# Causal linear attention: running sums over pairs of even and odd tokens, the even token's own term added from GpSimd

## The reference

```python
q, k = _rope(q, k); q = _phi(q); k = _phi(k)          # phi(x) = elu(x) + 1
def step(carry, qkv):
    K_sum, KV = carry
    q_t, k_t, v_t = qkv
    K_sum = K_sum + k_t
    KV = KV + k_t[..., :, None] * v_t[..., None, :]
    num = jnp.einsum('bhd,bhde->bhe', q_t, KV)
    den = jnp.maximum(jnp.einsum('bhd,bhd->bh', q_t, K_sum), EPS)
    return ((K_sum, KV), num / den[..., None])
```

## Time and profile before

| | us |
|---|---|
| median of 3 runs | 368.7 (367.78 to 368.82) |
| the profiled execution: its own time | 367.48 |
| its span | 365.7 |
| TensorE busy | 347.7 (95%) |
| VectorE busy | 317.6 (87%) |
| ScalarE busy | 276.1 (75%) |
| GpSimd busy | 204.3 (56%) |

### The profile page before, as it was taken

How to read it: one execution, slowest core, us unless ns; L and a number is a source line. 1 busy time by engine, 2 the same in 40 slices (tenths; PEclk the granted TensorE clock), 3 DMA queues, 4 the chain that set the end, 5 groups by cost and what they waited for, 6 DMA issues and landing times.

```text
span 365.7 us, 9318 instructions
## 1 busy us (share of the span) xinstructions
PE 347.7 (95%) x2534; PEld 299.9 (82%) x2534; DVE 317.6 (87%) x623; ACT 276.1 (75%) x774; POOL 204.3 (56%) x239
## 2 busy tenths in 40 slices
PE   7999988799899999999999899999999899999986
PEld 2788534499799999999999799989989688788875
DVE  3998799559989999999699979998996799998665
ACT  3887967777686877787878767787895987778752
POOL 3899118844234465756665648675857448883110
PEclk9999999999999999999999999999999999999999
DMA  6842848555355555655654554756642102221112
GB/s 182 217 124 74 325 192 234 173 149 134 108 133 137 139 143 146 170 139 150 175 143 135 152 161 129 186 150 152 148 115 70 31 2 57 57 61 29 30 29 59
DMA packets 45521, 47.00 MB, mean 129 GB/s; under 512 B 6928, under 2 KB 33712, under 8 KB 45216
## 3 DMA queue, kind: packets, MB, share of 16 engines
q1 hardware_dynamic: 40288, 36.88, 33.6%
q0 software_dynamic: 4320, 8.86, 11.5%
q10 hardware_dynamic: 864, 0.67, 0.7%
HBM read 32.88 MB, written 13.50 MB: 127 GB/s over the span
## 4 chain that ended last, share of the span: by engine, by line
PE 76%; DVE 14%; issue 3%; ACT 3%; DMA 2%; ACTq 1%; DVEq 0%
PE banks L546 16%; PE banks L534 14%; PE banks L674 6%; PE banks L675 6%; PE banks L330 3%; PE banks L983 3%; PE banks L1010 2%; PE banks L299 2%; PE banks L524 2%; PE banks L1039 2%; PE banks L321 2%; PE banks L1019 2%; PE banks L993 2%; PE banks L1057 2%; DVE cq L686 2%
## 5 line engine op out<-in xcount | busy, mean ns | idle before, releaser
L468 POOL DMA_INDIRECT xg<-xn_rows,slot_tok x71 | 74.8, 1053 | 74.2 <-PE banks L524 61.7
L563 ACT ACTIVATE xT<-banks,b1T 128x128 f32<-128x128 f32 x284 | 81.1, 371 | 15.4 <-PE banks L534 14.7
L546 PE MATMUL banks<-w_sb,xT 128*128 x568 | 79.6, 283 | 0.0
L485 POOL DMA_INDIRECT qk_exp<-expert_rows,ranki x64 | 63.7, 996 | 21.6 <-issue 17.9
L534 PE MATMUL banks<-xgT,w 128*128 128x128 f32 x568 | 75.3, 276 | 0.0
L546 PEld LDWEIGHTS banks<-w_sb,xT 128*128 128x128 f32 x568 | 69.3, 192 | 1.2
L534 PEld LDWEIGHTS banks<-xgT,w 128*128 128x128 f32 x568 | 69.0, 192 | 0.0
L686 DVE TENSOR_TENSOR cq<-banks,phi 128x360 f32<-128x360 f32 (+1 forms) x96 | 47.4, 548 | 19.1 <-PE banks L675 18.9
L652 ACT CAST high<-outer 128x1152 fp32r<-128x1152 f32 x32 | 37.1, 1158 | 21.6 <-DVE outer L641 21.2
L658 DVE TENSOR_TENSOR low<-outer,high 128x1152 fp32r<-128x1152 f32 x32 | 43.3, 1352 | 3.2 <-ACT high L652 3.2
L695 DVE TENSOR_REDUCE sums<-cq 128x144 f32<-128x1152 f32 x32 | 42.9, 1341 | 0.0
(11 more groups left out here) (205 smaller groups left out, 702.7 us busy)
## 6 DMA issues: line engine op xcount, KB each, us to landing
w<-in_L_ffn_W SPq DMA_DIRECT2D x71, 256.0 KB
expert_rows<-ye SPq DMA_DIRECT2D x71, 64.0 KB
expert_rows<-x_sb SPq DMA_DIRECT2D x2, 2048.0 KB, 10.6
x_sb<-in_L_attn_x SPq DMA_DIRECT2D x8, 256.0 KB, 4.3
xn_rows<-xn SPq DMA_DIRECT2D x8, 256.0 KB, 2.3
w_sb<-in_L_ffn_W SPq DMA_DIRECT2D x8, 256.0 KB, 4.5
out<-outer SPq DMA_DIRECT2D x7, 256.0 KB, 2.3
xg<-xn_rows,slot_tok POOLq DMA_INDIRECT x71
```

Source lines behind the costliest of these rows:

```text
L468: pool.indirect_dma_start(out=xg[n][:, :], out_offset=None, in_=xn_dram, in_offset=bass.IndirectOffsetOnAxis(ap=slot_tok[:, j:j + 1], axis ...
L485: pool.indirect_dma_start(out=y_moe[:, i, k, :], out_offset=None, in_=y_dram, in_offset=bass.IndirectOffsetOnAxis(ap=ranki[:, 0, k, i:i + ...
L546: last = nc.tensor.matmul(y, hidT[p][:, c, :], w2_sb[:, ds(e * NC + c, 1), :], start=False, stop=(c == NC - 1))
L563: last = nc.scalar.activation(hidT[p][:, c, :], ps[3 + p][:, c * P:(c + 1) * P], ACT.Gelu_apprx_tanh, bias=b1T[:, ds(e * NC + c, 1)])
```

## The change

Tokens are dealt out in pairs. Partition p of batch b now holds tokens 2p and 2p + 1: tile 2b has the even tokens, tile 2b + 1 the odd ones. The outer products of both are added (`attn_pair`), and there is one `high` and one `low` per batch, of that pair sum. An odd token needs all pairs up to its own: `tri_r`, 6 matmuls. An even token needs all pairs ahead of its own, `tri_x`, 6 matmuls, and its own product alone. That last part is (q . k) times (v, 1), which GpSimd computes in five small instructions (`attn_own`, into one of two buffers) and VectorE adds to the even tile's reduced sums (`attn_add_own`).

The feature map `phi` of the next batch moves from the end of the odd tile into the even tile's step, as do both outer products and the pair sum; `low` moves behind the sums of the odd tile. `high` is issued in the odd tile's step. x, its normalised copy and the output are moved by DMA with a pair of tokens in one line (1024 bytes where it was 512). In the second layer the blocks of a batch are swapped (`block_of`) and `mix` takes four instructions instead of two. GpSimd's and VectorE's moments share semaphores between the layers.

```diff
+    put("token_no", n // 2 * T + 2 * row + n % 2 - TOK // 2)
...
+    def by_tile(a, b, n):
+        return a.rearrange("(b p r) d -> p b (r d)", p=P, r=2)[:, b:b + n, :]
...
     def attn_outer(v, b, r, p):
...
-            v.wait_ge(high_ready, b * 2 - 1 + r)
-            v.wait_ge(low_ready, b * 2 - 1 + r)
+            v.wait_ge(high_ready, b)
+            v.wait_ge(low_ready, b)
+            v.wait_ge(pair_ready, b)
...
-    def attn_high(act, b, r, p):
-        i = b * 2 + r
-        act.wait_ge(outer_ready, i + 1)
-        act.wait_ge(den_ready, i + 1)
-        if from_(b, 2 - r):
-            act.wait_ge(cum_ps, b * 2 - (0 if r else 2))
-        nc.scalar.copy(high[kept(r, p)], outer[r]).then_inc(high_ready, 1)
-
-    def attn_low(v, b, r, p):
-        v.wait_ge(high_ready, b * 2 + r + 1)
-        n = kept(r, p)
-        nc.vector.tensor_tensor(low[n], outer[r], high[n].bitcast(f32), ALU.subtract).then_inc(low_ready, 1)
+    def attn_pair(v, b):
+        v.wait_ge(outer_ready, 2 * b + 2)
+        v.wait_ge(den_ready, 2 * b + 2)
+        nc.vector.tensor_tensor(outer[0], outer[0], outer[1], ALU.add).then_inc(pair_ready, 1)
+
+    def attn_high(act, b, p):
+        act.wait_ge(pair_ready, b + 1)
+        if b >= 2:
+            act.wait_ge(cum_ps, 2 * b - 2)
+        nc.scalar.copy(high[p], outer[0]).then_inc(high_ready, 1)
+
+    def attn_low(v, b, p):
+        v.wait_ge(high_ready, b + 1)
+        nc.vector.tensor_tensor(low[p], outer[0], high[p].bitcast(f32), ALU.subtract).then_inc(low_ready, 1)
+
+    def attn_own(pool, b, p):
+        pool.wait_ge(phi_ready, b + 1)
+        if b >= 2:
+            pool.wait_ge(own_used, b - 1)
+        nc.gpsimd.tensor_tensor(own_qk[:, :], phib[p][:, 0, 0:D], phib[p][:, 0, D:2 * D], ALU.mult).then_inc(own_part, 1)
+        q = own_qk[:, :].rearrange("p (h d) -> p h d", d=DH)
+        n = 4 * b + 1
+        for half in (DH // 2, DH // 4):
+            pool.wait_ge(own_part, n)
+            nc.gpsimd.tensor_tensor(q[:, :, 0:half], q[:, :, 0:half], q[:, :, half:2 * half], ALU.add).then_inc(own_part, 1)
+            n += 1
+        pool.wait_ge(own_part, n)
+        nc.gpsimd.tensor_tensor(own_dot[:, :], q[:, :, 0], q[:, :, 1], ALU.add).then_inc(own_part, 1)
+        pool.wait_ge(own_part, n + 1)
+        pool.wait_ge(ones_ready, 1)
+        nc.gpsimd.tensor_tensor(own[p][:, :, :], own_dot[:, :].unsqueeze(2).broadcast_to([P, H, E9]),
+                                qkv3[:, 2 * b, 2 * D:NW].rearrange("p (e h) -> p h e", h=H), ALU.mult).then_inc(own_ready, 1)
+
+    def attn_add_own(v, b, p):
+        v.wait_ge(own_ready, b + 1)
+        v.wait_ge(sums_ready, 2 * b + 1)
+        nc.vector.tensor_tensor(sums[:, 0, :, :], sums[:, 0, :, :], own[p][:, :, :], ALU.add).then_inc(own_used, 1)
...
     def attn_cumsum(pe, b, r, p):
-        pe.wait_ge(low_ready, i + 1)
-        parts = [(tri_r, kept(r, p))] + ([(ones_r, kept(0, p))] if r else [])
+        pe.wait_ge(low_ready, b + 1)
+        w = tri_r if r else tri_x
...
-            for m, (w, at) in enumerate(parts):
-                nc.tensor.matmul(o, w[:, :], high[at][:, cols], start=(m == 0), stop=False)
-                last = nc.tensor.matmul(o, w[:, :], low[at][:, cols], start=False, stop=(m == len(parts) - 1))
+            nc.tensor.matmul(o, w[:, :], high[p][:, cols], start=True, stop=False)
+            last = nc.tensor.matmul(o, w[:, :], low[p][:, cols], start=False, stop=True)
...
+    OWN_AT = [max(SUMS_AT[2 * b] - 3, 0) for b in range(B)]
...
     def mix(v, g, p):
         for m in range(2):
-            t = mix_t[p][m].rearrange("p (b t) -> p b t", t=T)
-            last = nc.vector.scalar_tensor_tensor(out=t, in0=xT2_of(p)[:, :, 0:T], scalar=one_mu[:, m:m + 1],
-                                                  in1=t, op0=ALU.mult, op1=ALU.add)
+            for lo, to in ((P + 1, 0), (0, P)):
+                t = mix_t[p][m].rearrange("p (b t) -> p b t", t=T)[:, :, to:to + P]
+                last = nc.vector.scalar_tensor_tensor(out=t, in0=xT2_of(p)[:, :, lo:lo + P], scalar=one_mu[:, m:m + 1],
+                                                      in1=t, op0=ALU.mult, op1=ALU.add)
...
         def _(act):
...
             def even(i):
+                if i % 2 and i + 1 < NT:
+                    attn_high(act, (i + 1) // 2, (i + 1) // 2 % 2)
...
             def odd(i):
-                if i + 2 < NT:
-                    attn_keys(act, i // 2 + 1, i % 2, 1 - i // 2 % 2)
-                    attn_high(act, i // 2 + 1, i % 2, 1 - i // 2 % 2)
+                if i % 2 == 0 and i + 2 < NT:
+                    for r in range(2):
+                        attn_keys(act, i // 2 + 1, r, 1 - i // 2 % 2)
...
         def _(pool):
...
+                if j in OWN_AT:
+                    attn_own(pool, OWN_AT.index(j), OWN_AT.index(j) % 2)
...
         def _(v):
...
                 attn_apply(v, b, r, p)
-                if i + 1 < NT:
-                    attn_low(v, (i + 1) // 2, (i + 1) % 2, (i + 1) // 2 % 2)
-                if till(b, B - 2):
-                    attn_outer(v, b + 1, r, 1 - p)
-                attn_sums(v, i, r)
-                if r == 1:
+                if r == 0:
+                    if b + 1 < B:
+                        phi(v, b + 1, 1 - p)
+                        for t in range(2):
+                            attn_outer(v, b + 1, t, 1 - p)
+                        attn_pair(v, b + 1)
+                    attn_sums(v, i, r)
+                else:
+                    attn_add_own(v, b, p)
+                    attn_sums(v, i, r)
+                    if b + 1 < B:
+                        attn_low(v, b + 1, 1 - p)
                     attn_reciprocal(v, b)
                     attn_divide(v, b)
-                if r == 1 and till(b, B - 3):
-                    phi(v, b + 2, p)
```

100 lines of the change are left out of this document (52 added, 48 removed).

## The result

| | us |
|---|---|
| before, median of 4 runs | 368.56 (367.78 to 368.82) |
| after, median of 4 runs | 383.37 (382.88 to 383.86) |
| ratio | 1.0405, 95% interval 1.0384 to 1.0427 |
| the profiled execution after: its own time, its span | 383.3, 381.5 |
| TensorE, VectorE, ScalarE, GpSimd busy | 335.6 (88%), 329.0 (86%), 261.7 (69%), 257.6 (68%) |

The change makes the kernel 4% slower, 14.8 us by the medians. Between the two profiled executions it is 383.3 - 367.48 = 15.8. The forecast said slower, by 8.2. (Some executions of a kernel fall into a slower state; the ratios given in this document leave them out.)

A forecast was written before the change was run, and what follows sets the result against it. TensorE was taken to pace each batch, with VectorE having 0.4 of slack in 12.04. Stage +2.0, collisions +5.2 and second layer +1.0 made +8.2: 375.7 from 367.48, 376.9 from the median, so 376, range 370 to 384.

The forecast's parts named there:

- loop: Expert stage: low, even cumsum and even apply wait on each other in turn; 12.80 us per batch, against 12.04 before.
- collisions: VectorE's two-source instructions held up by GpSimd's own terms: 0.4 in 13 of 15 gaps, +5.2 us, between 0 and 23.
- TensorE saves 1.07 per batch and waits for `low`: Odd cumsum: 6 matmuls for 12, so TensorE's work falls to 10.97 us per batch, then waits 1.8 for low.
- VectorE's own work, 12.08: Expert stage: VectorE's work per batch without any wait for the cumsum, including about 0.1 each for two dependent neighbours: 12.08 us.
- rival C: Expert stage: the wait between low and apply hides, batches fall to 12.08, kernel faster at 362 us; chance 0.13.
- as work they lie beside the gathers: GpSimd in the expert stage: gathers and returning rows 9.9 us, 11.9 with own terms and gaps, under 12.8 per batch.
- Rival E: GpSimd becomes the bound: own terms up to 5.5 us, 15.4 per batch in the last eleven; 395 to 400; chance 0.06.
- its counter-argument: Against GpSimd as the bound: once late, the own terms fall under VectorE's sums and are quick again.
- no cost: ScalarE: one high fewer per batch (1.16 us); the other ends near 7.0, long before low at 10.04.
- mix, +1.0: Second layer: four VectorE instructions for two, 0.16 us by six groups, +1.0; 0 to 1.7.
- Rival B: The loop stands, but GpSimd's instructions cost VectorE no time: 370.5 to 371.7 us, up to 373.5; chance 0.21.
- tiles 0 to 2: Start of the expert stage, tile 0 to 2: 14.19 us before, 13.5 after, so -0.7.

The follow-up runs named there:

- the memsets: The changed kernel with GpSimd's five own-term instructions replaced by five memsets that read nothing (the even tokens' own term a constant): 383.14 us.
- the control: The changed kernel as it is, measured again in a later group where the kernel before took 368.21: 382.95 us.

## Why the prediction was right in kind and short in size

It forecast 376.0 within 370 to 384, and slower with 0.80; 383.37 lies inside, near the upper edge, but the change is +15.8 between the profiled executions and not +8.2. Direction, loop and collisions were foreseen. What was not is that GpSimd's list had no room. Step by step:

**TensorE saves 1.07 per batch and waits for `low`:** right. The odd cumsum runs from 149.58 to 150.72, 1.14, and 1.14 of waiting stand ahead of the even one, where 1.8 was forecast; 0.55 more is a wait for `ye` in the same batch. Its busy share is 88% and was 95%.

**VectorE's own work, 12.08:** 12.34 in the run in which nothing waits. The bubbles behind a needed result are larger than I counted: 0.13 ahead of outer (0.81 - 0.68) against 0.03, and 1.45 from the even tile's sums to the odd apply against 1.37. This also settles rival C. With the loop hidden the batch is 12.34, not 12.08, and the kernel is no faster than before even without the own terms.

**The loop, 12.80 (12.5 to 13.1):** 13.03, from those bubbles and a hand-over between `low`'s end at 156.74 and the apply at 158.20 of 1.46 against 1.41. Its cost is shown: 8.8 us, the run with both causes removed against the one with the own terms alone removed. (With the own terms in place, `low` early wins 2.0.) Of the +9.0 from tile 2 to 20, 8 x 13.04 + 13.66 - 111.10 = 6.9 are the loop, forecast 4.3.

**Collisions, 0.4 in 13 of 15 gaps, +5.2:** the mechanism stands, the size doesn't. They cost 0.57 each, but only in three batches (13.60 where the clean one is 13.03) and 0.4 in the one ahead of them, because from tile 10 on, with the rows coming back in its list, GpSimd reaches them later and most of them fall beside sums and apply. That makes 2.1 between tiles 2 and 20. The forecast named this escape and still counted it as the rarer case. The Trainium skill ("SBUF — State Buffer", "Who interferes with whom") says that a VectorE instruction with two SBUF inputs contends with a GpSimd instruction that reads SBUF and not with one that only writes it. The own terms and the memsets in the same place agree with both halves: 2.93 and 2.36.

**GpSimd's list, "as work they lie beside the gathers":** this is the step that failed. I added 9.9 for the gathers and about 2 for the own terms, 11.9, and called it hidden under 12.8. Two things were wrong in it. The gathers are longer in the new order: from tile 10 to 20, 1.19 each on average where they took 0.97 before, so that with the issue gaps ahead of them they make 10.5 per batch. And the own terms take 2.1 there, with 0.2 of gaps, and not 1.8. Together that is 12.8 in batches of 13.2, which leaves 0.4 of waiting per batch where there were 3.6. (The 4.6 that the own terms take in the early batches did not hurt the list: GpSimd still waits 15.9 for others between 90.94 and 145.17.) The reserve of 61.7 fell to 19.3, and from tile 20 on, where deviations come in as well, nothing is left: between tile 22 and 30 GpSimd waits for others for 1.5 in 59.8 us. The lateness costs about 5 of the 6.8 that separate the kernels with and without own terms. Rival E had the place and the consequence (TensorE waits for xg), but by another way, own terms of 5.5 in the last eleven batches, with 395 to 400 and a chance of 0.06; from tile 10 to 24 they take 1.8 to 2.2, as its counter-argument said. What came was a mild form of it, most of it in one batch (17.02 against 13.04), which no case of mine held. It lies between tiles 22 and 30, 59.84 where the forecast was 53.9 + 1.2 for three collisions; without the own terms it is 55.18, so that 1.3 of the miss are the loop's and 3.5 come with the own terms. Of these 3.5, 1.6 are the clock at 0.50 in the profiled execution. The forecast had no term for the clock, since it was at its full level in the kernel before, where TensorE was busy for 38.5 to 40 of every 40 us from 80 to 280.

**ScalarE, "no cost":** wrong in one place. One `high` per batch waits behind the normalisation, which waits for GpSimd's deviation; there it delays `low` by 0.59 and, with the late slots and the lower clock, the apply by 3.75.

**mix, +1.0 (0 to 1.7):** +1.3 in the changed kernel, +1.5 by itself.

**Rival B, no collisions, 370.5 to 373.5:** the memsets are near that case, with time on GpSimd kept, and they take 383.14. Taking the collisions away wins nothing in the medians, though part of that is the clock; in the slower setting, moving the own terms out of the collisions won about 10.

By terms: the loop was 2.6 short, the collisions 1.5 too much between tiles 2 and 20, the late batches 4.8 short, the start 0.6 and tiles 0 to 2 0.8, mix 0.3. That is the 7.6 between 8.2 and 15.8. That the time still lies inside the range is in part luck: the range reached 384 to hold collisions beyond 0.4 per batch, and what filled it was GpSimd's list.

## What to carry to other kernels

When work goes to an engine that "has room", compare its reserve (how long it waits because it is ahead) with the new time, in the fullest stretch and not in the average one, and count that its old instructions may get longer too. Here 11.9 on paper was 12.8, and a reserve of 61.7 became 19.3. Before two times of one batch are compared, look at the granted clock in it. And before halving an engine's work, ask when its inputs are ready: the kernel before had each `low` a tile ahead of its reader, and giving that up turned 1.07 saved into 1.0 lost per batch.

## What the runs showed of the hardware

- A GpSimd instruction of 16 elements took 0.22 alone, and 1.29 to 1.43 where it started while VectorE ran an instruction with two SBUF sources; VectorE lost 0.57 over two such instructions. GpSimd lost more.
- A gather on GpSimd took 0.94 in most cases, and 1.65 to 2.1 in eight of 37 between tiles 10 and 20, all begun while VectorE ran an outer product or `low`; a few others begun beside these were shorter.
- Memsets of 600 elements on GpSimd (0.60 each) beside the same VectorE instructions stretch neither.
- With TensorE's granted clock at 0.50 for 3.4 us a slot and a cumsum took 4.86, at 0.50 for 6.8 us (the memsets) 5.65, and at 1.00 3.25. Ahead of the drop of 3.4 us TensorE was busy for 1.18 and 0.58 of two stretches of 2 us; with 1.20 and 0.79 in the same place the control kept 1.00.
- The same kernel took 368 in some groups of runs and 383 in others, the changed one 383 and 410. The traces of the changed kernel in the two settings agree up to tile 8 (131.56 and 131.74) and part soon behind the first gather of returning rows (129.9). The granted clock does not explain it: the kernel before had 0.987 to 1.0 in the groups where it took 383 to 385, and 0.991 to 1.0 where it took 368. Nor do the DMA transfers take longer as a whole, as two expectations suppose: the packets of the two busiest queues take 29.5% and 8.8% of 407.7 us against 31.9% and 9.6% of 381.5. GpSimd's reserve is no smaller (22.3), TensorE's waits for `ye` grow from 11.4 to 29.2, and 19.3 of VectorE's waits ahead of an apply have no releaser in the trace. The first of these applies starts at 147.11, 1.95 behind the row that follows its cumsum, where it was 0.20. What makes this stays open.
